# Windowed attention scores: one 64-row product per head, even and odd heads in a bank each

## The reference, cut to what matters

```
# 16 heads of 64, windows of 32 tokens
q, k, v = split(shift_tokens(x) @ Wqkv)
q, k = l2norm(q) * qs, l2norm(k) * ksc ; rotary on both
# query window w sees key windows w-1 and w (64 keys), masked
sim = einsum('bhwie,bhwje->bhwij', q, k2) * 8 ; softmax
out = einsum('bhwij,bhwje->bhwie', attn, v2)
x = out @ Wo + x ; then the feed-forward
```

## Time and profile before

| | |
|---|---|
| device time, median of 3 runs | 3595.3 us (3594.93 to 3595.39) |
| profiled execution, first to last instruction | 3598.4 us |
| PE busy | 3482.8 us, 97% |
| PE weight loads busy | 2390.4 us, 66% |
| DVE busy | 3160.0 us, 88% |
| ACT busy | 3061.0 us, 85% |
| POOL busy | 2352.0 us, 65% |
| mean granted TensorE clock | 0.998 |

### The profile page before, as it was taken

How to read it: one execution, slowest core, us unless ns; L and a number is a source line. 1 busy time by engine, 2 the same in 40 slices (tenths; PEclk the granted TensorE clock), 3 DMA queues, 4 the chain that set the end, 5 groups by cost and what they waited for, 6 DMA issues and landing times.

```text
span 3598.4 us, 95666 instructions
## 1 busy us (share of the span) xinstructions
PE 3482.8 (97%) x33868; PEld 2390.4 (66%) x33868; DVE 3160.0 (88%) x5848; ACT 3061.0 (85%) x5121; POOL 2352.0 (65%) x1607
## 2 busy tenths in 40 slices
PE   8999899999999999999999999999999999999998
PEld 6777466666666666666666666666666666666666
DVE  6998889888988988888888898888889888888986
ACT  5766688888888888888888888888888888888886
POOL 2001677777777777777777677777777777777774
PEclk9999999999999999999999999999999999999999
DMA  2000011112211112211112111112111112211112
GB/s 63 0 0 0 21 34 39 38 33 54 52 34 34 39 36 52 50 40 33 34 40 53 46 39 38 32 36 58 47 33 39 38 33 55 52 33 34 39 37 54
DMA packets 182965, 136.67 MB, mean 38 GB/s; under 512 B 97612, under 2 KB 135632, under 8 KB 182800
## 3 DMA queue, kind: packets, MB, share of 16 engines
q1 hardware_dynamic: 180019, 125.00, 14.8%
q10 hardware_dynamic: 2781, 9.51, 0.9%
HBM read 19.04 MB, written 2.10 MB: 6 GB/s over the span
## 4 chain that ended last, share of the span: by engine, by line
PE 62%; ACT 19%; issue 10%; DVE 5%; SPq 1%; POOL 1%; DMA 1%; ACTq 0%; DVEq 0%; POOLq 0%
PE ps L1302 12%; PE ps L1389 10%; PE ps L1356 10%; PE ps L1344 7%; PE ps L1379 4%; PE ps L1370 4%; PE ps L1160 3%; ACT L750 3%; ACT area L603 2%; DVE area L987 2%; ACT G L609 2%; ACT L609 2%; ACT area L618 2%; ACT area L625 2%; PE ps L1295 2%
## 5 line engine op out<-in xcount | busy, mean ns | idle before, releaser
L1302 PE MATMUL ps<-Wqkv,xsT 128*128 128x512 f32 x2304 | 1112.5, 605 | 8.7 <-ACT area L638 3.8
L449 POOL TENSOR_TENSOR area<-area,tab 128x512 f32<-128x512 f32 x768 | 970.0, 1273 | 146.7 <-ACT area L618 146.1
L1302 PEld LDWEIGHTS ps<-Wqkv,xsT 128*128 128x128 f32 x2304 | 391.2, 189 | 351.4 <-issue 295.0
L462 POOL TENSOR_TENSOR area<-area,lsum 128x1024 f32<-128x1024 f32 x192 | 365.5, 1904 | 383.2 <-DVE lsum L916 383.2
L456 POOL TENSOR_TENSOR AQb<-AQb,area 128x1024 f32<-128x1024 f32 x192 | 455.2, 2371 | 15.1
L456 POOL TENSOR_TENSOR area<-area 128x1024 f32<-128x1024 f32 x192 | 455.0, 2370 | 9.0 <-DVE area L976 1.5
L618 ACT ACTIVATE area<-ps 128x1024 f32<-128x1024 f32 x384 | 393.6, 1025 | 66.2 <-PE ps L1302 55.1
L1389 PEld LDWEIGHTS ps<-kbd,area 128*32 128x32 f32 x12288 | 313.2, 109 | 196.1 <-issue 113.4
L1344 PE MATMUL ps<-BD,area 128*64 128x128 f32 x6144 | 421.5, 279 | 17.7 <-issue 11.3
L1344 PEld LDWEIGHTS ps<-BD,area 128*64 128x64 f32 x6144 | 329.4, 137 | 158.8 <-issue 100.2
L1389 PE MATMUL ps<-kbd,area 128*32 128x128 f32 x12288 | 415.6, 276 | 17.0 <-ACT kbd L648 5.7
(11 more groups left out here) (136 smaller groups left out, 6630.6 us busy)
## 6 DMA issues: line engine op xcount, KB each, us to landing
BD<-area SPq DMA_DIRECT2D x1344, 64.0 KB, 2.0
Vx<-area SPq DMA_DIRECT2D x384, 32.0 KB, 1.9
Wqkv<-ffn_Wqkv ACTq DMA_DIRECT2D x18, 512.0 KB, 4.0
BB<-area SPq DMA_DIRECT2D x384, 16.0 KB, 1.8
x2s<-x2s SPq DMA_DIRECT2D x96, 56.0 KB, 2.0
Wo<-ffn_Wo SPq DMA_DIRECT2D x6, 512.0 KB, 4.3
W<-ffn_W SPq DMA_DIRECT2D x6, 341.0 KB
x2s<-x2s SPq DMA_DIRECT2D x96, 0.2 KB, 1.7
```

The costliest lines, as they stand in the source:

```text
L449: pool.tensor_tensor(b4[:, :, here], q4[:, :, there], s4[:, :, here], ALU.mult).then_inc((s_bq, s_bk)[j], 1)
L462: pool.tensor_tensor(p3, p3, lsum[:, 1, :].unsqueeze(2).broadcast_to([P, HEADS, 2 * WIN]), ALU.mult).then_inc(s_pn, 1)
L1302: last = mm(PJ[:, b * 512:(b + 1) * 512], xsT[:, par, t * P:(t + 1) * P], Wqkv[:, w0:w0 + 512], start=True, stop=True)
```

## The change

`kbd` becomes `kT`, the turned keys as they are: one copy by ACT for each group in the place of two (L648 is gone). The scores of a tile are one call in the place of two: for each pair, each window and each head k of the pair, 64 rows (that head's half of the partitions) by 32 columns of `qT`, against 64 x 64 of `kT`. Even heads go to bank 0 of `SC` and odd heads to bank 1, so that both banks are complete only when the call ends; `s_sc` counts once for a tile. The order of heads in the scores, in `BD` and in `BB` is now that of `place(h)`. PE waits for both masks and both copies before the call, each with a wait of its own (`need_apart`, with the new semaphore `i_pe`). The lists of ACT, DVE, POOL and SyncE keep their order.

```
@@ -98,9 +98,9 @@
-        kbd = sb("kbd", [P, PAIRS, 2, WIN + SEQ])
+        kT = sb("kT", [P, PAIRS, WIN + SEQ])
         BD = sb("BD", [P, TILES, NWIN, HEADS, WIN])
-        BB = sb("BB", [P, 2, 4, 2, WIN])
+        BB = sb("BB", [P, 4, 4, WIN])
...
@@ -237,6 +237,9 @@
+
+        def place(h):
+            return (h % 2) * PAIRS + h // 2
...
@@ -310,10 +313,9 @@
-                    edge = PTr[t][0:WIN, 0, :, :].rearrange("p (g c k) i -> p g c (k i)", g=2, c=4)
+                    edge = PTr[t][0:WIN, 0, :, :].rearrange("p (e c) i -> p e c i", c=4)
                     for c in range(4):
-                        sp.dma_start(BB[32 * c:32 * c + 32, :, c, :, :].rearrange("p g k i -> p g (k i)"),
-                                     edge[:, :, c, :]).then_inc(d_bd[t], 16)
+                        sp.dma_start(BB[32 * c:32 * c + 32, :, c, :], edge[:, :, c, :]).then_inc(d_bd[t], 16)
...
@@ -641,16 +643,14 @@
                 need(act, s_tr[g], turn_of_k(n, t))
-                need(act, s_sc, 4 * n - 1 + g)
-                c = slice(4 * g, 4 * g + 4)
+                need(act, s_sc, 2 * n)
                 at = slice(WIN + P * t, WIN + P * t + P)
-                act.activation(kbd[0:DH, c, 0, at], tr[0:DH], ACT.Copy)
-                act.activation(kbd[DH:P, c, 1, at], tr[DH:P], ACT.Copy).then_inc(s_te[g], 1)
+                act.activation(kT[:, 4 * g:4 * g + 4, at], tr, ACT.Copy).then_inc(s_te[g], 1)
             def q_evac(n, t, g):
                 need(act, s_tr[g], turn_of_q(n, t))
-                need(act, s_sc, 2 * T - 1 + g)
+                need(act, s_sc, T)
                 act.activation(qT[:, 4 * g:4 * g + 4, :], TR[g][:, :].rearrange("p (c n) -> p c n", c=4),
...
@@ -897,7 +897,7 @@
             def row_max(n, t, g):
-                need(dve, s_sc, 2 * T + g + 1)
+                need(dve, s_sc, T + 1)
...
@@ -1342,12 +1342,12 @@
-                                  BD[:, t, :, h, :], start=(c == 0), stop=False, skip_group_check=True)
+                                  BD[:, t, :, place(h), :], start=(c == 0), stop=False, skip_group_check=True)
-                                  BB[:, g, :, k, :], start=False, stop=True, skip_group_check=True)
+                                  BB[:, 2 * k + g, :, :], start=False, stop=True, skip_group_check=True)
...
@@ -1379,16 +1379,20 @@
-            def scores(n, t, g):
-
-                need(pe, s_mk, 4 * n + 2 * t + g + 1)
-                need(pe, s_te[g], turn_of_k(n, 1) if t else turn_of_q(n, 0))
-                for c in range(4 * g, 4 * g + 4):
+            def scores(n, t):
+
+                ready = turn_of_k(n, 1) if t else turn_of_q(n, 0)
+                need_apart(pe, i_pe, s_mk, 4 * n + 2 * t + 2)
+                need_apart(pe, i_pe, s_te[0], ready)
+                need_apart(pe, i_pe, s_te[1], ready)
+                for c in range(PAIRS):
-                        last = mm(SC[32 * w:32 * w + 32, g, (c % 4) * P:(c % 4 + 1) * P],
-                                  qT[:, c, 32 * w:32 * w + 32], kbd[:, c, :, k0:k0 + 2 * WIN],
-                                  start=False, stop=True, skip_group_check=True)
+                        for k in range(2):
+                            half = slice(DH * k, DH * k + DH)
+                            last = mm(SC[32 * w:32 * w + 32, k, 2 * WIN * c:2 * WIN * (c + 1)],
+                                      qT[half, c, 32 * w:32 * w + 32], kT[half, c, k0:k0 + 2 * WIN],
+                                      start=False, stop=True, skip_group_check=True)
                 last.then_inc(s_sc, 1)
...
@@ -1439,12 +1443,10 @@
                     values(n - 2, 1, 1, par)
-                if mid:
-                    scores(n - 1, 0, 0)
                     output(n - 2, 1)
-                    scores(n - 1, 0, 1)
+                    scores(n - 1, 0)
                     turn_q(n - 1, 1, 0)
                     turn_q(n - 1, 1, 1)
                     turn_k(n - 1, 1, 0)
...
@@ -1455,7 +1457,6 @@
                 if mid and not head:
                     unread(5)
                 if mid:
-                    scores(n - 1, 1, 0)
                     turn_k(n - 1, 1, 1)
                 if head:
                     if first:
...
@@ -1464,7 +1465,7 @@
-                    scores(n - 1, 1, 1)
+                    scores(n - 1, 1)
```

More of the change, by code:

```diff
@@ L139, in build @@
         nmx = sb("nmx", [P, 2, HA])
-        names = ("d_x d_x2 d_wa d_wap d_rot d_c d_wq d_wk d_wv d_qks d_wo d_ln d_ff d_out i_const i_zero i_pad i_dve i_pool i_sp i_guess i_bits d_id d_wav d_hm "
+        names = ("d_x d_x2 d_wa d_wap d_rot d_c d_wq d_wk d_wv d_qks d_wo d_ln d_ff d_out i_const i_zero i_pad i_dve i_pool i_sp i_guess i_bits i_pe d_id d_wav d_hm "
                  "a_lnc a_lnr a_lnn a_xh a_xt a_xe a_qk a_qe a_ke a_km a_v a_ve a_s a_mx a_e a_t a_te "
@@ L149, in build @@
         S = {n: sem(n) for n in names.split()}
-        (d_x, d_x2, d_wa, d_wap, d_rot, d_c, d_wq, d_wk, d_wv, d_qks, d_wo, d_ln, d_ff, d_out, i_const, i_zero, i_pad, i_dve, i_pool, i_sp, i_guess, i_bits, d_id, d_wav, d_hm,
+        (d_x, d_x2, d_wa, d_wap, d_rot, d_c, d_wq, d_wk, d_wv, d_qks, d_wo, d_ln, d_ff, d_out, i_const, i_zero, i_pad, i_dve, i_pool, i_sp, i_guess, i_bits, i_pe, d_id, d_wav, d_hm,
          a_lnc, a_lnr, a_lnn, a_xh, a_xt, a_xe, a_qk, a_qe, a_ke, a_km, a_v, a_ve, a_s, a_mx, a_e, a_t, a_te,
@@ L373, in _ @@
             pool.memset(x2s[:, :, :, :], 0.0).then_inc(i_zero, 1)
-            pool.memset(BB[:, :, :, :, :], 0.0).then_inc(i_zero, 1)
+            pool.memset(BB[:, :, :, :], 0.0).then_inc(i_zero, 1)
             pool.wait_ge(d_hm, 16)
@@ L393, in a_step @@
                     if isinstance(n, int) and n == 0:
-                        pool.memset(kbd[:, :, :, :], 0.0).then_inc(i_zero, 1)
+                        pool.memset(kT[:, :, :], 0.0).then_inc(i_zero, 1)
                         pool.memset(BD[:, :, :, :], 0.0).then_inc(i_zero, 1)
```

## The result

The changed kernel takes 4237.5 us (median of 4 runs, 4227.3 to 4241.3), the kernel before, run beside it, 3595.4 us (3594.9 to 3596.6). The ratio is 1.178, 95% interval 1.176 to 1.180: 642 us slower. The forecast was 4065 us and the range 3940 to 4260. The sign and the chain of waits came out as forecast, and 173 us were missing from the sum. The profiled execution has a span of 4239.5 us.

A forecast was written before the change was run, and what follows sets the result against it. The prediction took PE, with work 97% of the span, as the bound. It added 373 us of waits, 76 us of clock and 20 us of program to 3595 us: 4064, rounded to 4065 us; range 3940 to 4260 us.

The forecast's parts named there:

- The work on PE: Score calls: two of 1.01 us a step in the place of four, so PE works 2.0 us less.
- The rival of 4255 us: Score calls: heads of a pair don't run side by side, each call 2.02 us, 192 us more; chance 0.13.
- Steps 1 to 5: Output projection through tile 1's scores and layer norm: waits make the step 3.93 us longer, 373 us over 95 steps.
- The clock: After the new wait ahead of L1285, PE runs at half clock: 0.8 us a step (bounds 0 and 1.27), 76 us.
- The program: PE's loop body grows by 512 instructions and jumps back wait for code: 20 us taken, bounds 0 to 60.
- the bound of 2 us for a packet: At each of the loop's 30 jumps back, PE waits 0 to 2 us for an instruction packet.
- Feed limit: Score calls: matmuls can't be fed faster than 32 ns each, a call 4.04 us, 576 us more, 4640 us; chance 0.06.
- more instruction packets than the longer program has: Sign of being wrong, in the instruction queue: packets beyond the longer program's, whose loop body was put at 7.2 against 5.1.
- a call of 2 us: Sign of being wrong, at the score calls: 2 us or more, from halves one after another or a feed limit.
- a PE idle share that stays near 3%: Sign of being wrong, over PE's span: the forecast chain through DVE's list is then not the one that binds.
- a call of about 1.1 us: Sign of being right, in PE's timeline: a score call of x128 takes about 1.1 us.
- a step 3.7 to 5.2 us longer: Sign of being right: from one L1285 to the next, 3.7 to 5.2 us more than before.

The follow-up runs named there:

- E2: The changed kernel with all even heads' products issued ahead of all odd heads' in a score call: 4366.2 us.
- E3: The changed kernel with DVE's layer norm work moved ahead of the first row maximum of tile 1: 3961.5 us.
- E1: The kernel before with its four score calls merged into two at the change's places, one signal a tile, old products and copies kept: 4269.9 us, ratio 1.187.
- E4: The changed kernel with 11 bf16 matmuls of 512 columns, results unread, ahead of the turned rows (L1285): 4179.0 us.
- E8: Hybrid: tile 0 as in the kernel before, tile 1 with the change's products in two halves, E3's order on DVE: 3650.0 us, ratio 1.015.
- E5: The changed kernel with the loop over the middle sequences written out, so no jump back there: 4217.7 us.
- E6: E3 with ACT's two copies of tile 1's turned queries ahead of the mask of tile 1's first half: 4016.3 us.

## Why the prediction was right, and where its sum was short

**The work on PE.** The sum took 1.01 us for a call of 128 matmuls. It is 1.42 us: half the length did not mean half the time. That is the mis-sized term behind the table above: L1370 comes 0.40 us later than forecast. At the second call the longer work makes DVE's maximum start 1.52 us behind the call's start instead of 1.15, the way from there to L1285 is 0.19 us shorter than taken, and L1285 comes 0.45 us late. The claim that two heads share the array was right (E2), but E2 also sizes it: one after another costs 0.40 us a call, not 1.01. The rival of 4255 us, heads one after another, was refuted as a mechanism, and its price was too high.

**Steps 1 to 5.** The chain binds as written: at every place the releaser is the one named, and the wait ahead of L1285 is 2.92 us against "some 3.1". The step is 4.4 us longer instead of 3.93 (37.46 against 33.05). Times 95 that is 418 us, not 373: 45 us of the missing 173. E3 takes the dearest point out and gives back 276 us, and E1, with the places alone, loses as much as the change. The chain is shown.

**The clock.** The term was 76 us, with 0.8 us a step. The changed kernel shows 78 of 95 steps with a slow stretch, 1.39 us each (38.85 against 37.46): 108 us. E1 gives 1.37 us with no late code in play. E4, which removes most of the stretches, wins only 58 us. So the term lies between 58 and 108 us and was fairly sized. A stretch of it in the changed kernel (window: length, PE busy, granted clock, DMA share, GB/s), with the one ahead of it, in which PE waits 2.97 us for L1285:

```profile
1600.00:1603.00 3.00, 1.20 (x4) 0.90 0.09 22
1603.00:1606.00 3.00, 3.00 (x6) 0.53 0.42 105
```

In the second PE is busy all through, nearly all of it at 1.2 GHz, as it was in the earlier trace rows.

**The program.** This is the term that failed: 20 us, with 60 as the upper bound. What steps and clock leave is 642 - 418 - 108 = 116 us. E1, which has the place without the longer code, leaves nothing, so I put the 116 us down to the code. Two losses make it up.

A jump back holds PE's sequencer for 3.3 to 4.3 us, 0.21 before: the bound of 2 us for a packet was too low for the branch itself. But work in hand covers most of it. PE stands idle for 37.8 us at the 30 jumps, 1.3 us each, and the step is longer by 1.1 us (39.97 against 38.85), by up to 2.0 where no slow stretch hides it (E4). That is 34 to 60 us: inside the bound and in its upper half, where the prediction took the lower third with no row behind it.

Code also arrives late inside the calls, and this the prediction put at nothing without a word: 33 of the 192 calls take 1.7 to 3.8 us from their first start to their last, the others 1.27. Such a step is 2.7 us longer without a jump (41.52 against 38.85, 14 steps) and 3.5 us with one (43.48 against 39.97, 10 steps): some 72 us. No run isolates it.

The Trainium skill (Runtime: NRT & Kernel Launch, Instruction fetch mechanics) gives PE 2,048 instructions in blocks of 256 and says that a taken branch outside the window has to fetch first. The trace agrees that a long body is fetched again: 405 packets for one of 1,832 instructions in 7.2 blocks, 126 for one of 1,570 in 6.1 (E8) and 98 for one of 1,310 in 5.1. The page's window is of two blocks only; with that the trace disagrees, since the bodies of 5.1 and 6.1 blocks would not fit into it. That text pointed at the upper half of the bound, and it should have moved the term.

**Feed limit.** The Trainium skill (TensorE: Matmul & The Clock Gate, the section on 56 ns) states a floor of some 25 ns from start to start. The trace disagrees for tiles of the array that differ: the 128 matmuls of a call start within 1.27 us, 9.9 ns each.

**What would have shown it wrong.** One of the signs named, more instruction packets than the longer program has, did appear, and it marks the term that was short. The others, a call of 2 us or a PE idle share that stays near 3%, did not. Two of the signs of being right were missed: a call of about 1.1 us in the timeline (it is 1.49), and a step 3.7 to 5.2 us longer. The undisturbed step is 4.4 us longer, but the median of all 95 is 39.46 us, 6.4 longer.

**What was luck.** With every term at its upper bound the forecast's own sum is 3595 + 373 + 121 + 60 = 4149 us. The measured 4237.5 us lie 88 us above it. They lie in the range because the range was drawn up to 4260 for heads one after another, which is not what happened.

**What stays open.** How much of the clock's loss lies under other waits in each step, why E5 has more slow clock than the change, and what exactly makes code late inside the calls.

## What to carry to other kernels

A piece of work on the busiest engine may be worth more as cover than it costs: before it is made shorter or joined with another, look at what the next entry of the list waits for, and at what in the other engines' lists stands *behind* an entry that waits for the joined work. Where a layout makes a call need two buffers at once, price the place that forces, not the instructions it saves. And count the body of a loop before a finer product is written out: here the step from 1,570 to 1,832 instructions turned 126 packets into 405, and the code's loss was some 116 us.

## What the runs showed of the hardware

- 128 matmuls of 64 rows, 32 columns of the array and 64 elements start within 1.27 us. The old form's 32 of 128 rows and 128 elements take 1.01 us to the successor. Twice the matmuls at half the length for the same scores: 0.77 us for what took 1.01 (E8).
- With a loop body of 1,832 PE instructions a jump back held PE's sequencer for 3.3 to 4.3 us (0.21 with 1,310) and lengthened the step by 1.1 to 2.0 us. Calls with waits inside came besides; writing the loops out did not cure them (E5: 32 waits, 56.5 us).
- An idle PE costs twice: E4 spends busy work on nothing and is 58 us faster; E6 joins two waits into one and is 55 us slower at about the same sum of waits and the same undisturbed step, with 282 us at half the clock in the place of 99.
